# Which engine's queue issues the pair-table blocks of the six edge passes

## The chip, the cores and the metric

The program runs on one core of a Trainium2 chip. The metric is the device time of one execution in microseconds, from launch to the last output. The engines are TensorE (PE), VectorE (DVE), ScalarE (ACT), GpSimd (POOL) and SyncE (SP), which only moves data and waits. SP and ACT issue plain DMAs; POOL issues the indirect ones. All of them move through the same 16 DMA engines.

## The reference, cut to what matters

A graph of 12,500 nodes with 128 features and 200,000 edges, sorted by destination, goes through four layers, each followed by a residual and a layer norm:

```python
x = layernorm(x + L0(x, edges, w))          # W x + b, weighted neighbour sums
x = layernorm(x + L1(x, edges, attr))       # features of edges beside those of sources
x = layernorm(x + L2(x, edges, w))          # two weighted SAGE layers
x = layernorm(x + L3(x, edges, types))      # three GRU steps: msg = (h @ W_et[type])[src]; a = segment_sum(msg, dst)
```

Behind the first layer there are six sums over all edges: one for L1, two for L2, three for L3. Each is one pass below.

## The kernel before, in words

**A pass.** Each of the six passes (`ph` 1 to 6) sums rows of a table in DRAM over the edges. Most edges go by gathers. A turn has four quarters `q` of four chunks with 128 edges each. ACT copies four index columns into `stage` (line 1253) and raises `staged`; POOL issues four indirect gathers of 128 rows (line 1068), one for each column; DVE builds one-hot matrices (line 2159); PE multiplies the gathered rows by them (line 1653) and raises `summed`; DVE adds the sum to `acc` (line 2136). There are two sets of gather buffers, of even and odd turns, so ACT's copy for quarter `q` of turn `t` waits until PE has summed quarter `q` of turn `t - 2`. The profiled input takes 71 turns.

**Pair blocks.** The edges of the most frequent destinations were added earlier into two pair tables in DRAM (`PAIR_BLOCKS`), as dense weights from source tiles to groups of destinations. A pass multiplies them on PE in 196 units. A unit is one of 98 tiles of 128 source nodes and one of two halves of the table. Six units (three tiles) go with two turns: `unit(p, c)`, `c` 0 to 5. In PE's order quarter 0 is followed by no unit, quarters 1, 2 and 3 by one each. In passes 4 to 6 a unit has a block of 1 MB and four 128x512 products (line 1634), and there are two block buffers, one for each half. In passes 1 to 3 it has one field of the table, 256 KB in pieces of 256 bytes, one product (line 1637), and six buffers. Each tile also needs its rows of the node table (`dense_t` or `dense_x`). PE raises `dense_done` behind each unit.

**Who issues.** SP issues the blocks and the rows in `unit_rows` (lines 722 to 738), each behind a wait on `dense_done`. The same queue holds the loads and stores of the per-node steps (lines 801 to 842), each behind its own wait, and in pass 1 the edge features `rec` (line 743), behind waits on `summed`. All these stand in one fixed order: in passes 4 to 6 the store of types of an earlier step is ahead of unit 0 of the next pair of turns. In pass 1, blocks are asked for one turn ahead of that. At the end of a pass SP waits for all its stores before it issues the first blocks of the next.

**What stands on ACT.** ACT's order in `stage_pass` (line 1247) is four index copies a turn and, behind copies 0, 1 or 2 of some turns, the activations of a node step: `gates` (lines 1347 and 1348) behind copy 0, `new_state` (line 1353) behind copy 1, square roots behind copy 2. Before a pass ACT already waits until the table of that pass is stored.

Of the kernel before, what the change touches and what calls it, by code (L numbers as in the profile page):

```python
# [14 lines left out]
P = 128  # L15
D = 128
DE = 32
KT = 4
# [16 lines left out]
HALF = P // 2  # L35
# [61 lines left out]
def build(nc, x, src, dst, edge_attr_32, edge_type_4, edge_weight, L0_gnn_W, L0_gnn_b, L1_gnn_u, L1_gnn_W1,  # L97
# [4 lines left out]
    with ctx:  # L102
# [479 lines left out]
        def _(sp):  # L582
# [139 lines left out]
            def unit_rows(ph, table, p, c):  # L722

                half, tile = c % NH, c // NH
                unit = p * (NH * TILES) + ((ph - 1) * UNITS + c)
                at = bass.ds((p * TILES + tile) * P, P)
                if ph > 3:
                    wait(sp, dense_done, unit - 1)
                    sp.dma_start(dense_b[:, half, :, :], PAIR_BLOCKS[half][at, :, 0:KT * HALF]).then_inc(dense_in[c], 16)
                else:  # L730
                    field = (F_ONE if ph == 1 else F_W) * HALF
                    wait(sp, dense_done, unit + (1 - NH * TILES) if not isinstance(p, int) else max(unit + (1 - NH * TILES), (ph - 1) * UNITS))
                    sp.dma_start(dense_w[:, c, :, :], PAIR_BLOCKS[half][at, :, field:field + HALF]).then_inc(dense_in[c], 16)
# [12 lines left out]
            def features_in(t, unit=None):  # L746

                edge = slot_regs(mybir.EngineType.SP, edge_row, t, EP - GE)
                for q in range(NQ):
                    feature_rows(t, q, edge)  # L750
                    if unit is not None and q:
                        unit(q - 1)

            def stream_pass(ph, table, load, store, late=None):

                def body(p, units):

                    for a in range(2):
                        if a == 0 and not (isinstance(p, int) and p == 0):
                            load(p - 1)  # L760
                        if a == int(ph < 4) and not (isinstance(p, int) and p < 2):
                            store(p - 2)

                        def unit(i):
                            if a * TILES + i < units:
                                unit_rows(ph, table, p, a * TILES + i)

                        def next_unit(i):
                            if a == 0:
                                if TILES + i < units:  # L770
                                    unit_rows(ph, table, p, TILES + i)
                            elif not isinstance(p, int) or p < LEAD:
                                unit_rows(ph, table, p + 1, i)
                        if ph == 1:
                            features_in(p * 2 + a, next_unit)
                        else:
                            for i in range(TILES):
                                unit(i)
                    if late is not None and not (isinstance(p, int) and p < 2):
                        late(p - 2)  # L780
                if ph == 1:
                    for i in range(TILES):
                        unit_rows(ph, table, 0, i)
# [20 lines left out]
            def layer_pass(ph, k, loads, table, into, late=None):  # L804

                def load(m):
                    src_ = step_of(mybir.EngineType.SP, m, (NG - 1) * GN, step_src)
                    wait(sp, step_free, before(total, k, m))
                    for slot, t_ in loads:
                        sp.dma_start(by_tile(slot), node_rows_of(t_, src_)).then_inc(step_in, 16)  # L810
# [5 lines left out]
                stream_pass(ph, table, load, store, late)  # L816
                sp.wait_ge(step_out, total * (16 * (k + 1)))

            layer_pass(1, 0, [(s_xin, X1)], X1, X2)
            layer_pass(2, 1, [(s_xin, X2)], X2, H1)  # L820
# [6 lines left out]
            layer_pass(3, 2, [(s_xin, H1), (s_yin, X2)], H1, X3, types_store)  # L827
            for hh in range(2):
                sp.wait_ge(first_out[hh], total * 16)

            def state_pass(n):
# [12 lines left out]
                stream_pass(4 + n, TT[n % 2], load, store)  # L844
                if n < 2:
                    for hh in range(2):
                        sp.wait_ge(types_out[hh], total * (16 * (n + 1)))
            for n in range(3):
                state_pass(n)

# [237 lines left out]
        def _(act):  # L1088
# [158 lines left out]
            def stage_pass(ph, index, k, parts, late=None):  # L1247

                def turn(t, par, part=None, places=parts):
# [10 lines left out]
                def body(p, units):  # L1260
                    if isinstance(p, int) and p < 2:
                        turn(p * 2, 0)
                        turn(p * 2 + 1, 1)
                        return
                    g = step_of(mybir.EngineType.Activation, p - 2)
                    turn(p * 2, 0, step_parts(p - 2, g))
                    if late is None:
                        turn(p * 2 + 1, 1)
                    else:
                        turn(p * 2 + 1, 1, lambda q: late[q](p - 2, g), late)  # L1270
# [61 lines left out]
            stage_pass(1, meta_src, 0, {0: rows_turned(True), 2: step_root()})  # L1332
            act.wait_ge(step_out, total * 16)
            stage_pass(2, meta_src, 1, {0: rows_turned()})
# [6 lines left out]
            stage_pass(3, meta_src, 2, {0: rows_turned(), 2: step_root()}, {0: state_kept})  # L1341
# [13 lines left out]
            for n in range(3):  # L1355
# [5 lines left out]
                stage_pass(4 + n, meta_row, n, {0: gates, 1: new_state})  # L1361
# [1081 lines left out]
```

## Time and profile before

| | |
|---|---|
| runs | 14902.51, 14829.66, 14875.42 us; median 14875.42 |
| profiled execution | 14825.95 us |
| its span | 14824.3 us |
| granted TensorE clock, mean | 0.761 |
| DMA queue of SP (q1) | 2403570 packets, 1628.59 MB |
| indirect DMAs of POOL (q0) | 447568 packets, 628.96 MB |
| DMA queue of ACT (q10) | 31722 packets, 15.04 MB |

The page gives busy times, the waits who waited for whom, and the timeline the instructions in order of time, neighbours of one line merged. A DMA issue is a row of the queue (SPq, ACTq) and is not counted as busy; its duration is that of the issue, not of the transfer. In a merged row the duration runs from the first start to the last end, so two issues with a pause between them show the pause. "remote" is a release that the trace can't put down to an instruction. Ends of matmuls are modelled.

### The profile page before, as it was taken

To read this page: it belongs to the slowest core of one execution; us is meant where nothing else is said; L and a number is where in the kernel's file an instruction comes from. 1 tells how busy PE (TensorE), PEld (TensorE's weight loads), DVE (VectorE), ACT (ScalarE), POOL (GpSimd) and SP (SyncE) were. 2 spreads that over 40 slices of the span, in tenths; PEclk is the share of its full clock that TensorE was granted. 3 is DMA by queue.
4 is the path that set the end of the run, shared out by engine and by line. 5 is a ranking of instruction groups with operands and counts; after the bars stand their busy time and mean duration, and the time that the engine had idled before them with its cause. 6 is when DMAs were issued, how large, how long until landed. Compare 5 with 4: busy or idle time off the path is not lost. (4 is left out here: it accounts for less than half of the span.)

```text
span 14824.3 us, 166292 instructions
## 1 busy us (share of the span) xinstructions
PE 9912.4 (67%) x37230; PEld 6043.2 (41%) x37231; DVE 4854.0 (33%) x18913; ACT 1607.7 (11%) x4318; POOL 9042.1 (61%) x8448
## 2 busy tenths in 40 slices
PE   5777777886677665444445554788867888577775
PEld 3444443226545443333333333344433444344443
DVE  3333334552322222222233333233332333322224
ACT  1111112222100000000000000111100000000001
POOL 2888888770366565666656665666656666566662
PEclk6555556778777776666667777899988999788887
DMA  8999998998534332333334443666646666366663
GB/s 283 220 221 221 223 221 114 115 117 193 126 94 99 90 95 71 92 91 91 83 95 119 115 117 95 187 209 207 211 128 197 209 206 213 122 190 187 190 190 92
DMA packets 2883133, 2275.44 MB, mean 153 GB/s; under 512 B 1211014, under 2 KB 2655107, under 8 KB 2882796
## 3 DMA queue, kind: packets, MB, share of 16 engines
q1 hardware_dynamic: 2403570, 1628.59, 37.2%
q0 software_dynamic: 447568, 628.96, 22.0%
q10 hardware_dynamic: 31722, 15.04, 0.4%
q8 instruction: 76, 1.25, 0.0%
q14 instruction: 197, 1.61, 0.0%
HBM read 1545.67 MB, written 755.00 MB: 155 GB/s over the span
## 5 line engine op out<-in xcount | busy, mean ns | idle before, releaser
L1634 PE MATMUL bank<-work 128*128 128x512 f32 x4704 | 2312.7, 636 | 581.5 <-DMA work<-t_pairs 345.3
L1068 POOL DMA_INDIRECT ring<-t_types,stage x1728 | 1669.9, 966 | 1239.3 <-ACT stage L1253 727.9
L2136 DVE TENSOR_TENSOR acc<-acc,bank 128x128 f32 x1704 | 487.4, 286 | 5402.6 <-remote 3824.9
L1043 POOL DMA_INDIRECT t_sums<-ring,stage x1136 | 1763.1, 1552 | 455.5 <-issue 273.0
L1068 POOL DMA_INDIRECT ring<-t_x,stage x1152 | 1119.9, 972 | 1410.4 <-ACT stage L1253 1071.0
L1634 PEld LDWEIGHTS bank<-work 128*128 128x128 f32 x4704 | 910.2, 204 | 1579.0 <-issue 1124.1
L1653 PE MATMUL bank<-ring 128*128 128x128 f32 x6912 | 1123.2, 307 | 574.0 <-issue 418.0
L1653 PEld LDWEIGHTS bank<-ring 128*128 128x128 f32 x6912 | 1046.8, 220 | 922.9 <-issue 797.5
L1068 POOL DMA_INDIRECT more_rows<-t_types,stage x840 | 798.6, 951 | 373.4 <-issue 256.1
L2159 DVE TENSOR_SCALAR ring<-iota_f,meta_low 128x128 f32<-128x128 f32 x4544 | 1001.4, 292 | 0.1
L1514 PE MATMUL bank<-aux 128*128 128x128 f32 x2272 | 528.8, 408 | 572.7 <-ACT aux L1193 560.7
L1637 PE MATMUL bank<-work 128*128 128x512 f32 x1176 | 742.8, 711 | 139.6 <-issue 139.1
L1057 POOL DMA_INDIRECT t_pairs<-acc,pair_stage x440 | 690.3, 1569 | 230.8 <-issue 100.8
L1068 POOL DMA_INDIRECT ring<-t_h,stage x576 | 556.6, 966 | 349.3 <-ACT stage L1253 187.6
L1514 PEld LDWEIGHTS bank<-aux 128*128 128x128 f32 x2272 | 473.0, 308 | 701.1 <-ACT aux L1193 656.6
L2159 DVE TENSOR_SCALAR ring<-iota_f,meta_low,meta_w 128x128 f32<-128x128 f32 x2272 | 660.5, 360 | 250.1 <-issue 248.5
L2034 DVE SCALAR_TENSOR_TENSOR aux<-bank,aux,upto 128x128 f32<-128x128 f32 x1136 | 331.0, 349 | 1192.7 <-PE bank L1499 1004.0
L1068 POOL DMA_INDIRECT more_rows<-t_x,stage x560 | 543.3, 970 | 265.7 <-issue 164.9
L1653 PE MATMUL bank<-ring,more_rows 128*128 128x128 f32 x3360 | 521.2, 306 | 268.7 <-issue 226.8
L1653 PEld LDWEIGHTS bank<-ring,more_rows 128*128 128x128 f32 x3360 | 492.4, 220 | 393.2 <-issue 385.6
L1564 PE MATMUL bank<-work 128*128 128x448 f32 x880 | 553.0, 717 | 120.2 <-DVE aux L2076 99.7
L1253 ACT ACTIVATE stage<-meta_src 128x4 uint32 (+1 forms) x852 | 167.6, 206 | 4199.1 <-remote 2702.3
(319 smaller groups left out, 14712.1 us busy)
## 6 DMA issues: line engine op xcount, KB each, us to landing
work<-t_pairs SPq DMA_DIRECT2D x588, 1024.0 KB
t_pairs<-acc SPq DMA_DIRECT2D x544, 648.0 KB
work<-t_pairs SPq DMA_DIRECT2D x588, 256.0 KB
t_types<-work SPq DMA_DIRECT2D x216, 512.0 KB
work<-t_types SPq DMA_DIRECT2D x294, 256.0 KB
aux<-t_pairs SPq DMA_DIRECT2D x196, 256.0 KB
work<-t_x SPq DMA_DIRECT2D x108, 256.0 KB
ring<-t_types,stage POOLq DMA_INDIRECT x1728
```

The costliest lines, as they stand in the source:

```text
L1043: pool.indirect_dma_start(TAB[k], bass.IndirectOffsetOnAxis(ap=stage[:, u:u + 1], axis=0), msg[:, u, :], None, compute_op=ALU.add).then_in ...
L1057: pool.indirect_dma_start(PAIR_ROWS[TABLE_OF[s]], bass.IndirectOffsetOnAxis(ap=pair_stage[:, u:u + 1], axis=0), pair_out[:, u, :], None, c ...
L1068: pool.indirect_dma_start(gathered[par][u], None, table, bass.IndirectOffsetOnAxis(ap=stage[:, par * U + u:par * U + u + 1], axis=0)).then ...
L1253: act.activation(stage[:, at:at + K], cols(index, t * U + q * K, K), ACT.Copy).then_inc(staged, 1)
L1514: mm = pe.matmul(bank[4 + q][:, k * P:(k + 1) * P], dups[:, q, k * P:(k + 1) * P], wx_rows[:, q, :], start=True, stop=True)
L1564: pe.matmul(o[:, 0:ROW], pair_eqs[:, r, :], pair_hot[:, r, :], start=True, stop=True)
L1634: mm = pe.matmul(o, dense_t[:, tile, k_ * D:(k_ + 1) * D], dense_b[:, half, :, k_ * HALF:(k_ + 1) * HALF], start=first and k_ == 0, stop=e ...
L1637: mm = pe.matmul(o, dense_x[:, tile, :], dense_w[:, c, :, :], start=first, stop=end)
L1653: mm = pe.matmul(bank[q][:, 0:P], gathered[par][u], hot[:, u, :], start=k_ == 0, stop=k_ == K - 1)
L2034: ins = v.scalar_tensor_tensor(out=eqs[:, u, :], in0=bank[2 + q % 2][:, k * P:(k + 1) * P], scalar=cols(srcs, c + k, 1), in1=upto[:, :], o ...
L2136: v.tensor_tensor(into, into, bank[q][:, 0:P], ALU.add).then_inc(added, 1)
L2159: ins = v.tensor_scalar(hot[:, q * K + k_, :], iota_f[:, :], low(c + k_), weight(c + k_) if weight else None, ALU.is_equal, ALU.mult if we ...
```

## The change

`unit_rows` leaves SP. ACT gets `block_rows` with the same transfers and semaphores, called from `turn` behind index copies 1, 2 and 3 (not behind copy 0, and ahead of the node-step part of the same quarter). The slots are chosen so that the buffer of the issued block is the one that PE's unit frees at the time of that copy: in passes 1 to 3 ACT issues unit `c` of pair `p` at its own turn, in passes 4 to 6 the unit two further on. The rows of passes 1 to 3 go behind the second half's block, with no wait of their own. In passes 4 to 6 the first two blocks and one set of rows go ahead of the first index copy. SP keeps loads, stores and edge features, and no longer waits for all stores at the end of each pass; the load of the first step of passes 2 and 3 waits for them, and one wait stands behind all passes.

```diff
-            def unit_rows(ph, table, p, c):        # on SP, called in turns with load, store, feature_rows
...
-                if half == 0:
-                    if ph < 4:
-                        wait(sp, dense_done, unit - 4 if not isinstance(p, int) else max(unit - 4, (ph - 1) * UNITS))
-                    sp.dma_start(dense_t[:, tile, :] if ph > 3 else dense_x[:, tile, :], table[at, :]
-                                 ).then_inc(dense_x_in[tile], 16)
...
+                def block_rows(p, c):
+                    half, tile = c % NH, c // NH
+                    unit = p * (NH * TILES) + ((ph - 1) * UNITS + c)
+                    at = bass.ds((p * TILES + tile) * P, P)
+                    if ph > 3:
+                        wait(act, dense_done, unit - 1)
+                        act.dma_start(dense_b[:, half, :, :], PAIR_BLOCKS[half][at, :, 0:KT * HALF]).then_inc(dense_in[c], 16)
+                    else:
+                        field = (F_ONE if ph == 1 else F_W) * HALF
+                        wait(act, dense_done, unit + (1 - NH * TILES) if not isinstance(p, int) else max(unit + (1 - NH * TILES), (ph - 1) * UNITS))
+                        act.dma_start(dense_w[:, c, :, :], PAIR_BLOCKS[half][at, :, field:field + HALF]).then_inc(dense_in[c], 16)
+                    if half == int(ph < 4):
+                        act.dma_start(dense_t[:, tile, :] if ph > 3 else dense_x[:, tile, :], table[at, :]
+                                      ).then_inc(dense_x_in[tile], 16)
...
+                def blocks_ahead(p, a, units, before_):
+                    def block(i):
+                        if ph < 4:
+                            c = a * TILES + i
+                            if c < units:
+                                block_rows(p, c)
+                        else:
+                            c = a * TILES + i + NH
+                            if c < NH * TILES:
+                                if c < before_:
+                                    block_rows(p - 1, c)
+                            elif c - NH * TILES < units:
+                                block_rows(p, c - NH * TILES)
+                    return block
...
                         act.activation(stage[:, at:at + K], cols(index, t * U + q * K, K), ACT.Copy).then_inc(staged, 1)
+                        if block is not None and q:
+                            block(q - 1)
                         if part is not None and q in places:
                             part(q)
```

## Rows read from the trace of the kernel before

**Rows 1.** The page's first part: busy us, share of span, instructions.

```profile
PE 9912.4 (67%) x37230; PEld 6043.2 (41%) x37231; DVE 4854.0 (33%) x18913; ACT 1607.7 (11%) x4318; POOL 9042.1 (61%) x8448
```

**Rows 2.** Windows, the six passes: stretch, length, busy us and counts, clock, DMA share.

```profile
3862.00:5682.00 1820.00, 1248.32 (x6041) 882.89 (x6042) 504.98 (x2270) 115.34 (x412) 1118.50 (x1136) 0.73 0.39 92
...
5748.00:7439.00 1691.00, 709.31 (x3308) 533.81 (x3308) 455.90 (x1616) 90.21 (x347) 1080.46 (x1136) 0.67 0.36 89
...
11090.00:12816.00 1726.00, 1342.91 (x4484) 721.80 (x4484) 523.98 (x1737) 116.16 (x382) 1090.77 (x1136) 0.90 0.63 197
...
sum 10384.00, PE 6774.97 PEld 4156.39 DVE 3090.24 ACT 765.24 POOL 6557.55; mean PE 1129.16 PEld 692.73 DVE 515.04 ACT 127.54 POOL 1092.93
```

**Rows 3.** Waits of all engines over the passes: us in total, times, longest.

```profile
POOL ring L1068 <- ACT stage L1253: 1986.6, 333, 532.2
...
PE bank L1634 <- DMA work<-t_pairs: 345.3, 88, 13.7
POOL more_rows L1068 <- ACT stage L1253: 256.8, 102, 4.4
POOL work L1068 <- ACT stage L1253: 254.5, 67, 5.3
POOL wT L1068 <- ACT stage L1253: 190.8, 56, 5.2
PE bank L1634 <- DMA work<-t_types: 131.4, 50, 10.0
...
PE bank L1649 <- DMA rec<-sorted_attributes: 32.1, 24, 3.4
```

**Rows 4.** Sources L729 and L737, SP's issues: ns min/median/max, starts.

```profile
L729 SPq DMA_DIRECT2D work<-t_pairs x588: 3/554/1325, 9281.8 to 14495.4; - x196
...
L737 SPq DMA_DIRECT2D work<-t_types x294: 2/517/3081, 9282.4 to 14492.2; - x147
```

**Rows 5.** Timeline, pass 4: start us, us, engine, line, count, idle before.

```profile
10203.53 5.92 SPq L729 DMA_DIRECT2D work<-t_pairs  x2
10203.54 0.21 ACT L1253 ACTIVATE stage<-meta_w 128x4 uint32 x1 [12.83 <-remote]
...
10204.55 0.99 POOL L1068 DMA_INDIRECT wT<-t_types,stage  x1 [3.50 <-ACT stage L1253]
...
10224.68 3.87 SPq L729 DMA_DIRECT2D work<-t_pairs  x2
...
10227.84 0.21 ACT L1253 ACTIVATE stage<-meta_w 128x4 uint32 x1 [14.20 <-remote]
...
10238.44 0.56 SPq L729 DMA_DIRECT2D work<-t_pairs  x1
...
10240.91 2.84 SPq L842 DMA_DIRECT2D t_types<-work  x2
...
10244.84 3.70 PE L1634 MATMUL bank<-work 128*128 128x512 f32 x8 [1.22 <-DMA work<-t_pairs]
...
10245.17 0.01 SPq L729 DMA_DIRECT2D work<-t_pairs  x1
```

**Rows 6.** Timeline, pass 2, same columns.

```profile
6299.85 7.16 SPq L733 DMA_DIRECT2D work<-t_pairs  x2
...
6301.02 0.95 POOL L1068 DMA_INDIRECT more_rows<-t_x,stage  x1 [0.30 <-issue]
...
6317.99 0.21 ACT L1253 ACTIVATE stage<-meta_src 128x4 uint32 x1 [14.27 <-remote]
...
6319.28 0.20 ACT L1253 ACTIVATE stage<-meta_src 128x4 uint32 x1
```

**Rows 7.** Waits of SP's queue, whole span.

```profile
SPq L842 <- DVE work L2393: 330.4, 15, 76.4
```

**Rows 8.** Timeline, ACT's weight loads at the start.

```profile
1.35 0.46 ACTq L1095 DMA_DIRECT2D ring<-in_L_gnn_W1l  x1
```

More of the change, by code:

```diff
@@ L744, in feature_rows, with features_in @@
                              S_ATTR[bass.ds(edge[q], GE), :].rearrange("(k p) f -> p k f", p=P)).then_inc(attr_in[q], 16)
-            def features_in(t, unit=None):
+            def features_in(t):
                 edge = slot_regs(mybir.EngineType.SP, edge_row, t, EP - GE)
@@ L750, in features_in, with stream_pass @@
                     feature_rows(t, q, edge)
-                    if unit is not None and q:
-                        unit(q - 1)
-            def stream_pass(ph, table, load, store, late=None):
+            def stream_pass(ph, load, store, late=None):
                 def body(p, units):
@@ L762, in body @@
                             store(p - 2)
[L764 to L773, printed above, removed]
                         if ph == 1:
[L775 to L778, printed above, removed]
+                            features_in(p * 2 + a)
                     if late is not None and not (isinstance(p, int) and p < 2):
                         late(p - 2)
-                if ph == 1:
-                    for i in range(TILES):
-                        unit_rows(ph, table, 0, i)
                 pairs_of_turns(sp, body)
@@ L802, in stream_pass, with layer_pass @@
                     late(total - 1, True)
-            def layer_pass(ph, k, loads, table, into, late=None):
+            def layer_pass(ph, k, loads, into, late=None):
                 def load(m):
                     src_ = step_of(mybir.EngineType.SP, m, (NG - 1) * GN, step_src)
-                    wait(sp, step_free, before(total, k, m))
+                    if k and isinstance(m, int) and m == 0:
+                        sp.wait_ge(step_out, total * (16 * k))
+                    else:
+                        wait(sp, step_free, before(total, k, m))
                     for slot, t_ in loads:
@@ L815, in store @@
                     sp.dma_start(node_rows_of(into, g), by_tile(s_res)).then_inc(step_out, 16)
[L816 to L820, printed above, removed]
+                stream_pass(ph, load, store, late)
+            layer_pass(1, 0, [(s_xin, X1)], X2)
+            layer_pass(2, 1, [(s_xin, X2)], H1)
             def types_store(m, last_=False):
@@ L826, in types_store @@
                     sp.dma_start(node_rows_of(TT[0], g, slice(hh * 2, hh * 2 + 2)), by_tile(first_types[hh], 2)).then_inc(first_out[hh], 16)
-            layer_pass(3, 2, [(s_xin, H1), (s_yin, X2)], H1, X3, types_store)
-            for hh in range(2):
-                sp.wait_ge(first_out[hh], total * 16)
+            layer_pass(3, 2, [(s_xin, H1), (s_yin, X2)], X3, types_store)
             def state_pass(n):
@@ L843, in store @@
                                      ).then_inc(types_out[hh], 16)
[L844 to L847, printed above, removed]
+                stream_pass(4 + n, load, store)
             for n in range(3):
                 state_pass(n)
+            sp.wait_ge(step_out, total * 48)
             def to_out(at):
@@ L1245, in _, with stage_pass, turn @@
             total = all_steps(act)
-            def stage_pass(ph, index, k, parts, late=None):
-                def turn(t, par, part=None, places=parts):
+            def stage_pass(ph, index, k, table, parts, late=None):
+                def block_rows(p, c):
[18 more added lines that the diff above has]
+                                block_rows(p, c)
+                        else:
+                            c = a * TILES + i + NH
[5 more added lines that the diff above has]
+                    return block
+                def turn(t, par, part=None, places=parts, block=None):
                     for q in range(NQ):
@@ L1260, in body @@
                 def body(p, units):
+                    before_ = LAST_UNITS if isinstance(p, int) and p == LEAD + 1 else NH * TILES
+                    even, odd = (blocks_ahead(p, a, units, before_) for a in range(2))
                     if isinstance(p, int) and p < 2:
-                        turn(p * 2, 0)
-                        turn(p * 2 + 1, 1)
+                        if ph > 3 and p == 0:
+                            for c in range(NH):
+                                block_rows(0, c)
+                            even = odd = None
+                        turn(p * 2, 0, block=even)
+                        turn(p * 2 + 1, 1, block=odd)
                         return
                     g = step_of(mybir.EngineType.Activation, p - 2)
-                    turn(p * 2, 0, step_parts(p - 2, g))
+                    turn(p * 2, 0, step_parts(p - 2, g), block=even)
                     if late is None:
-                        turn(p * 2 + 1, 1)
+                        turn(p * 2 + 1, 1, block=odd)
                     else:
-                        turn(p * 2 + 1, 1, lambda q: late[q](p - 2, g), late)
+                        turn(p * 2 + 1, 1, lambda q: late[q](p - 2, g), late, block=odd)
                 pairs_of_turns(act, body)
@@ L1331, in _ @@
                 act.wait_ge(p_l0.st[par], p_l0.st_before[par] + 16 * (NG // 2 + 1 - par))
[L1332 removed]
+            stage_pass(1, meta_src, 0, X1, {0: rows_turned(True), 2: step_root()})
             act.wait_ge(step_out, total * 16)
[L1334 removed]
+            stage_pass(2, meta_src, 1, X2, {0: rows_turned()})
             def state_kept(m, g):
@@ L1360, in _ @@
                 gates.out = (lambda i: i * 16) if n < 2 else (lambda i: total * 32)
-                stage_pass(4 + n, meta_row, n, {0: gates, 1: new_state})
+                stage_pass(4 + n, meta_row, n, TT[n % 2], {0: gates, 1: new_state})
             def state_copy(at):
```

12 lines of the change are left out of this document (1 added, 11 removed).

## The prediction

> **What bounds the kernel now.** I read the busy shares first [rows 1]. No engine is full: PE has 67% of the span, POOL 61%, ACT, which gets the new work, only 11%. The windows by pass [rows 2] say more. The six passes are 10384.0 us of the 14824.3 us span, and the change touches nothing outside them. A pass takes 1691 us (pass 2), 1726 us (pass 5) or 1820 us (pass 1), although PE is busy for 709 us in pass 2 and 1343 us in pass 5. Twice the PE work moves the pass by 2%, so PE's arithmetic doesn't set the time. POOL's 1136 gathers are the same in each. One takes 0.95 us and has 0.30 us of idle before it [rows 6], so 1136 x 1.25 = 1420 us a pass, 8520 us in six. The rest, 10384 - 8520 = 1864 us, is time in which POOL issues nothing.
>
> The waits [rows 3] say for whom: POOL waited 333 times before `ring` gathers, 102 before `more_rows`, 67 before `work` and 56 before `wT`, 558 times, each time for ACT's index copy. A handful of those are starts of passes, and one of them is 532.2 us long, so I count 550 pauses. The timeline [rows 5] shows such a pause: the gather at 10204.55 had waited 3.50 us for the copy at 10203.54, and that copy had waited 12.83 us for a release that the trace can't name. By the code it is PE's `summed`. So the bound is a loop: PE sums a quarter, ACT copies, POOL gathers 1.25 us a chunk until its permits are used up, and it pauses until PE's next sums are told. A change counts in two places: if it lets PE finish a quarter sooner, or if it puts something between `summed` and the copy.
>
> **What is taken from SP.** 588 blocks of passes 4 to 6 at a median of 0.554 us and their 294 rows at 0.517 us [rows 4]; passes 1 to 3 have as many of each by the loops, 1176 blocks and 588 rows in all. SP's own time is worth nothing, as SP isn't in the loop. What can be worth something is the moment at which a block is issued.
>
> In passes 4 to 6 PE waited 345.3 us, 88 times, for a block, and 131.4 us for rows [rows 3], 476.7 us together. In passes 1 to 3, with six buffers, no such row is among the waits, so an earlier issue gives nothing there. The 476.7 us are the ceiling of this term and 0 is its floor. Most of it is transfer, not lateness. The block issued at 10238.44 was used at 10244.84, 6.40 us later, PE waiting 1.22 us for it [rows 5]; its issue took 0.56 us and nothing held it up, so ACT could not have made it come sooner. The other kind is seen at the same place: SP issued the two type stores from 10240.91 for 2.84 us, and the next block only at 10245.17, 1.42 us after their end. SP waits 330.4 us in all, 15 times, for the types of such a store [rows 7], and a block stands behind it; ACT has no stores. But the held block is unit 0, and PE has two quarters and the gate products to do before it uses that. I take a quarter of the ceiling, near the floor: 476.7 / 4 = 119 us saved.
>
> Pass 1 has one more: PE waited 32.1 us, 24 times, for edge features [rows 3], which SP issues in turns with blocks. With the blocks gone half may go, 16 us; floor 0, ceiling 32.
>
> **What is put on ACT.** A block issue is some 0.55 us, and with two or three register instructions I take 0.65 us; where rows go with it, 0.65 + 0.52 = 1.17 us. ACT's own issues at the start took 0.46 us for a smaller transfer [rows 8], so the price on ACT isn't higher than on SP. In total that is 1176 x 0.65 + 588 x 0.52 = 1070 us on an engine that is busy for 765 us of 10384 us in the passes [rows 2]. It fits easily. A turn has 20 us of gathers, and gets three blocks, 2 to 3 us.
>
> What counts is the order. Behind a block's wait and issue stand the next index copy, the step activations, and through the copy POOL. The wait itself costs nothing in principle, as the unit that frees the buffer stands ahead of the next quarter's sums in PE's order. The issue costs if permission for block and copy come together. Then the copy, for which POOL is paused, is late by 0.65 to 1.17 us. In [rows 5] SP's issue at 10203.53 and the copy at 10203.54 are such a case: they came at the same instant. At 10224.68 and 10227.84 the issue was 3.16 us ahead of the copy, and would have been over in time. And quarter 1 has no block ahead of its copy. Of 550 pauses the ceiling is all of them with rows, 550 x 1.17 = 644 us; the floor is 0. Between "half" (the two cases above) and "few" (one slot in four has no block, and blocks are freed a few us before the sums as a rule) I take a quarter: 550 / 4 x 0.65 = 89 us added. Where several permissions come together, as at 6317.99 and 6319.28, where two copies follow in 1.3 us [rows 6], only the first one matters: POOL has 5 us of gathers from each.
>
> The parts of the node steps: gates stand behind copy 0, where no block is; `new_state` stands behind block 0 of its turn, but PE forms the products it needs after the unit that frees that block, so the issue lies beside them: 0, and 0.65 us if that cover is missing, 108 times in all, 70 us.
>
> **Edges of passes.** In passes 4 to 6 two blocks and one set of rows go ahead of the first copy: 3 x (0.65 x 2 + 0.52) = 5 us. In passes 1 to 3 there are no such issues and the first blocks come later than from SP, but PE uses block 0 only after two quarters, 8 gathers or 10 us. SP's dropped waits at the ends are repeated by the wait that ACT has already: 0. Stores in SP's queue get free of blocks: they are not waited for by the loop, 0.
>
> **Sum.** -119 - 16 + 89 + 5 = -41 us against the profiled 14825.95 us, which gives 14785. That execution is 49 us below the median of the runs, 14875.42; against the median, -41 gives 14834, and I say 14835.
>
> The transfers themselves, bytes, pieces and DMA engines, stay as they are. The Trainium skill, "DMA: Bandwidth & Descriptors", section "Issuing engines are not separate DMA queues", says that DMAs from different issuing engines end up on the same 16 engines and that spreading the issue saves only the sequencer's time. By that rule the first term would be the part of the 476.7 us that is SP's lateness alone, as I have it; without it one would book the whole 476.7 us and forecast 14477. The use 6.40 us after a punctual issue [rows 5] agrees with the rule.
>
> **Rivals.** *SP is slow, and that is what PE feels.* In pass 2 two block issues took 7.16 us together [rows 6] while a single one has a median of 0.554 us [rows 4], and in the same stretch POOL and ACT go on at their usual durations. If blocks, rows and edge features come from a queue that doesn't stretch, most of PE's 476.7 + 32.1 us may go, and the pauses with them. For it: the 5.92 us and 3.87 us of pairs of issues in pass 4 [rows 5]. Against: an issue also looks late when PE's `dense_done` is told late, and ACT would see it as late; and pass 2, where SP stretches most, has no PE wait on blocks at all. Two thirds of 509 us less the 94 us of costs is -245, with a few pauses fewer -300: 14575 us.
>
> *The copies are late.* The slower side, by one mechanism: PE's releases come in bunches, so that block and copy are permitted together, as at 10203.53. If that is so at half of the pauses, and half of these blocks carry rows (mean 0.91 us), 275 x 0.91 = 250 us are added; with the block term at its floor and 5 us of edges the time is 14875 + 255 = 15130 us. It decides from about (119 + 16) / 0.91 = 150 delayed pauses, 27% of the 550. For it: the instant shared by both in one of the two cases. Against: the other case, and copy 1.
>
> *ACT gets as slow as SP.* If what stretches SP's issues comes with issuing, ACT takes 3.6 us instead of 0.65 us for a block (half of 7.16 us), 11 us a turn, and copies stand behind that. At 3 us a turn over 6 x 71 = 426 turns that is +1280 us: 16150 us. Nothing shows ACT stretched in these passes, but it issues nothing there.
>
> The Trainium skill, "Perfetto Trace Analysis", section on the HWDGE DMA instruction, has a rule that speaks against the change: the two issuing sequencers share one descriptor generator, which is locked for one of them at a time. SP's remaining stores and ACT's blocks could then hold each other up. No row here shows both queues issuing at once in a pass. It would make the second rival's price larger, by up to one issue.
>
> **Chances.** The forecast, own range 14740 to 14930: 0.46. SP's slowness 0.25, late copies 0.22, a slow ACT 0.04, the rest 0.03. I take 0.5% as what a measurement of this kernel can tell from no change; that is 74 us, so the line is at 14801 and 14950. The forecast gives 0.12 of its chance to faster, 0.31 to same and 0.03 to slower. With the rivals: faster 0.37, same 0.34, slower 0.29. The range for 8 in 10 reaches into both rivals, from 14510 to 15130.
>
> **What would show it.** In the profile after, q10 carries the blocks and rows and q1 the rest; the block issues are ACTq rows of 0.5 to 0.6 us. Right, if PE's waits for `t_pairs` fall from 345.3 by less than half, the passes stay within 1% of [rows 2], and POOL's waits for the copy stay near 550 with a little more length each. The first rival shows as PE's waits near 0 and shorter passes, pass 1 most. The second shows as POOL's pauses up by 0.5 us each with an ACTq issue right ahead of the copy. The third shows as ACTq rows stretched to microseconds. I am wrong as well if passes 1 to 3 move by over 1%, where I book almost nothing.

## The result, and the profile after

The kernel after takes 14951.74 us (median of 5 runs, 14938.77 to 14988.88), the kernel before 14868.64 us in the same comparison (14824.13 to 14902.51). The ratio is 1.0065, 95% interval 1.0046 to 1.0083. That is 83 us more by the medians, where 41 us less was forecast. Three further comparisons of the same two kernels gave 1.0054 [1.0036, 1.0072], 1.0055 [1.0038, 1.0071] and 1.0058 [1.0039, 1.0077]. The profiled execution after took 14957.69 us, its span is 14956.0 us.

The windows by pass of after, answering to [rows 2] (stretch, length, busy us and counts, clock, DMA share, GB/s; from a pass's first gather to its last):

```profile
3838.00:5687.00 1849.00, 1221.16 (x6052) 874.27 (x6052) 509.54 (x2287) 120.09 (x414) 1120.35 (x1136) 0.73 0.39 91
5748.00:7442.00 1694.00, 721.72 (x3308) 550.93 (x3308) 463.46 (x1619) 91.69 (x350) 1080.33 (x1136) 0.67 0.35 89
...
11178.00:12913.00 1735.00, 1353.88 (x4468) 725.08 (x4468) 523.46 (x1727) 115.41 (x377) 1089.09 (x1136) 0.89 0.63 196
...
sum 10541.00, PE 6801.67 PEld 4194.03 DVE 3094.64 ACT 772.01 POOL 6549.34; mean PE 1133.61 PEld 699.00 DVE 515.77 ACT 128.67 POOL 1091.56
```

The six passes are 10541.0 us against 10384.0 us: more than the whole loss is in them. PE has 0.4% more busy time and POOL 0.1% less; what grew is the time in which both wait. POOL's idle part is 10541 - 8520 = 2021 us by the count of the prediction, where it was 1864 us. Of the 157 us, 65 are in passes 1 to 3 (5291 us against 5226 us, 1.2%), which the prediction named as a sign of being wrong.

The sources of ACT's issues (ns min/median/max), answering to [rows 4]:

```profile
L1217 ACTq DMA_DIRECT2D work<-t_pairs x588: 547/561/649, 9318.5 to 14634.0; - x196
```

```profile
L1223 ACTq DMA_DIRECT2D work<-t_types x294: 536/541/1972, 9319.1 to 14624.9; - x147
```

The issue costs on ACT what was said, 0.561 and 0.541 us at the median. In passes 4 to 6 no block's issue takes over 0.65 us; single issues of rows take up to 1.97 us. The waits over the passes, answering to [rows 3]:

```profile
POOL ring L1029 <- ACT stage L1247: 1646.3, 357, 89.4
...
PE bank L1636 <- DMA work<-t_pairs: 416.6, 91, 15.2
...
POOL work L1029 <- ACT stage L1247: 272.8, 73, 5.2
...
POOL more_rows L1029 <- ACT stage L1247: 257.9, 90, 5.4
...
PE bank L1636 <- DMA work<-t_types: 156.5, 51, 6.7
...
POOL wT L1029 <- ACT stage L1247: 103.1, 27, 5.9
```

PE's waits for blocks did not fall from 345.3 us, they are 416.6 us; those for rows went from 131.4 to 156.5 us. These are single profiles: the three other profiles of the kernel after have 291.9 to 396.3 us for blocks, a second one of the kernel before (14711.06 us, on the chip called B below) 244.3 us, and 206.5 us for rows. Only the 32.1 us for edge features are gone. POOL's waits for a copy stay near 550 (357 + 73 + 90 + 27 = 547). Their sum can't be set against [rows 3] as it stands, as that holds one of 532.2 us at the start of the passes.

The timeline of after in pass 4 shows what is new (start us, us, engine, line, what, idle before; ACT and POOL, DVE's addition of a sum and PE's next unit):

```profile
9701.96 0.56 ACTq L1217 DMA_DIRECT2D work<-t_pairs  x1
9702.25 0.29 DVE L2138 TENSOR_TENSOR acc<-acc,bank 128x128 f32 x1 [7.55 <-remote]
...
9702.72 0.20 ACT L1247 ACTIVATE stage<-meta_w 128x4 uint32 x1 [8.99 <-remote]
9702.96 0.55 ACTq L1217 DMA_DIRECT2D work<-t_pairs  x1
...
9703.68 1.35 ACTq L1223 DMA_DIRECT2D work<-t_types  x1
9703.72 1.00 POOL L1029 DMA_INDIRECT work<-t_types,stage  x1 [4.38 <-ACT stage L1247]
...
9705.23 0.20 ACT L1247 ACTIVATE stage<-meta_w 128x4 uint32 x1 [2.31 <-issue]
...
9708.54 3.78 PE L1636 MATMUL bank<-work 128*128 128x512 f32 x4 [11.32 <-DMA work<-t_pairs]
```

POOL stood still for 4.38 us for the copy at 9702.72, and that copy began 0.20 us (register instructions) behind the end of a block's issue that began at 9701.96. The copy at 9705.23 again begins 0.20 us behind an issue, of rows, but POOL had four gathers to do and lost nothing by it. Where a copy ends a pause of over 1 us and its row follows on an ACT issue with nothing but register instructions between (0.2 us of them, in about a third of the cases 0.5 us), I call it held: in the profile after 88 are (24, 22 and 41 of them in passes 4, 5 and 6, one in pass 1), in the three other profiles of the same kernel 69, 84 and 69; in the kernel before, where ACT issues nothing, none. The issues ahead of them, with their register instructions, take 74 us, and 64, 78 and 67 us in the others. That is the most by which these copies can be late, as a copy's own release may have come while the issue ran. A count that asks for a copy to begin behind the issue's end, by 0.6 us at most, gives 81, 62, 73 and 61 (81, 64, 74 and 64 us), so the numbers are good to some 15%. Copies with a table load between issue and copy (last section) are not among them; that is 9 to 15 more in each profile, all in pass 4.

PE's 11.32 us in the last row are not all idle time. By the modelled ends PE's last sum was over at 9697.2, but ACT's issue was released only at 9701.96, and VectorE's next additions of sums begin at 9702.25 and 9703.23. So a sum of PE's waits in this document is an upper count, of the kernel before as well as of the others.

### The profile page after: what moved, and what is told of

Read it like the earlier page. It is cut to its first block and busy times, and to the rows that moved or that the text cites. A ratio compares the mean times of both kernels' runs of the same rounds, so it can differ in the third digit from the quotient of the medians.

```text
span 14956.0 us, 166227 instructions
## 1 busy us (share of the span) xinstructions
PE 9920.8 (66%) x37230; PEld 6075.6 (41%) x37231; DVE 4856.6 (32%) x18913; ACT 1612.5 (11%) x4318; POOL 9034.3 (60%) x8448
## 5 line engine op out<-in xcount | busy, mean ns | idle before, releaser
L1636 PE MATMUL bank<-work 128*128 128x512 f32 x4704 | 2356.5, 646 | 715.7 <-DMA work<-t_pairs 416.6
L1639 PE MATMUL bank<-work 128*128 128x512 f32 x1176 | 730.2, 702 | 73.5 <-issue 72.4
```

Source lines behind the costliest of these rows:

```text
L1636: mm = pe.matmul(o, dense_t[:, tile, k_ * D:(k_ + 1) * D], dense_b[:, half, :, k_ * HALF:(k_ + 1) * HALF], start=first and k_ == 0, stop=e ...
L1639: mm = pe.matmul(o, dense_x[:, tile, :], dense_w[:, c, :, :], start=first, stop=end)
```

## The experiments

Comparisons ran on three chips, here A, B and C. The kernel before takes 14827 to 14834 us on A, 14748 to 14862 us on B and 13032 us on C; each ratio below is against the kernel before on the same chip in the same comparison. There is no profile of the kernel before on C; what is said of C is read from profiles of four edited kernels. Here are the passes of the profiles on chip A, from the first gather of a pass to the first of the next (of pass 6 to its last gather), in us, worked out from the traces:

| kernel | 1 | 2 | 3 | 4 | 5 | 6 | 1 to 3 | 4 to 6 | ratio |
|---|---|---|---|---|---|---|---|---|---|
| waits alone on ACT | 1869 | 1734 | 1803 | 1811 | 1813 | 1700 | 5406 | 5324 | 1.0005 |
| ACT issues in 1 to 3 | 1888 | 1734 | 1824 | 1820 | 1802 | 1705 | 5446 | 5327 | 1.0016 |
| the change | 1894 | 1733 | 1827 | 1860 | 1820 | 1724 | 5454 | 5404 | 1.0055 |
| time on ACT, no wait | 1895 | 1740 | 1814 | 1816 | 1812 | 1711 | 5449 | 5339 | 1.0024 |
| double time behind waits | 1889 | 1740 | 1839 | 1863 | 1856 | 1735 | 5468 | 5454 | 1.0106 |
| copies first | 1881 | 1730 | 1827 | 1874 | 1861 | 1742 | 5438 | 5477 | 1.0124 |

Each row is one profile, and one kernel's profiles differ: in the four of the change, on A, B and the first comparison, passes 1 to 3 take 5401 to 5483 us and passes 4 to 6 take 5349 to 5410 us.

### Which passes

ACT issues for the passes in `ACT_PH` and SP for the others. SP's waits at the ends of passes (1 and 2, or 3 to 5) are dropped with it, as in the change.

```diff
             def unit_rows(ph, table, p, c):
+                if ph in ACT_PH:
+                    return
...
                 def block_rows(p, c):
+                    if ph not in ACT_PH:
+                        return
```

> The other half: ScalarE issues in passes 1 to 3 alone, SyncE in passes 4 to 6. Theory A: ratio 1.000 to 1.002, as only one pause there ends behind an issue. Theory B, and any cause that lies in passes 1 to 3: 1.003 or more. The two halves should add up to 1.0065 if passes are independent.

Measured on A: 14847.35 us against 14834.15 us, ratio 1.0016 [1.0002, 1.0029].

> ScalarE issues blocks and rows in passes 4 to 6 alone, SyncE in passes 1 to 3. The whole change costs 83 us (ratio 1.0065), and passes 1 to 3 alone came to 1.0016. Theory A (the issues stand between a release and an index copy, where PE has only two buffers, so in passes 4 to 6): 60 to 75 us, ratio 1.004 to 1.005, and 80 to 90 pauses of POOL that end with a copy right behind an ACT issue. Rival B (the block's transfer is served worse from ACT's queue): the same ratio, but the pauses behind an issue would not account for it, and PE's waits for t_pairs rise from 345 to over 400 us. If the cost is spread evenly over all passes: 1.003.

Measured on C, before at 13032.38 us: 13044.92 us, ratio 1.0006 [0.9997, 1.0015]. Once more, and the change itself, on B, before at 14748.0 us:

> ScalarE issues in passes 4 to 6 alone. Gave 1.0006 on the chip on which POOL never pauses. Where before takes about 14830 us, Theory A expects 1.004 to 1.005 (the whole change less the 1.0016 of passes 1 to 3) and some 88 pauses of POOL behind an ACT issue; where before takes 13030 us again, 1.0006 again.

> The change itself, once more. Two chips gave two different programs: on one (before 14834 us) POOL pauses some 80 times a pass and single SyncE and TensorE instructions take 0.7 us for long stretches; on the other (before 13032 us) POOL never pauses over 1 us and a pass takes 1390 us instead of 1680 us. Where before takes about 14830 us: 1.0065 again. Where it takes about 13030 us, Theory A (the issue costs only where POOL waits for the copy) expects 1.000 to 1.002; if the cost is in ACT's queue or in PE's waits for blocks it is 1.004 or more there too.

Measured: 14836.51 us, ratio 1.0059 [1.0039, 1.0080], with 77 held copies (82 us); the whole change in the same comparison 14834.17 us, 1.0054 [1.0036, 1.0072]. The expected rise of PE's waits for `t_pairs` to over 400 us, had ACT's queue served blocks worse, did not come here: they are 359.8 us. In the four profiles of the whole change they are 291.9 to 416.6 us, so this sign is a weak one; the next but one experiment tests the queue itself. By the ratios nearly all of the loss is from passes 4 to 6, where there are two block buffers. The two halves make 1.0075 together, more than the whole; the intervals allow it. This edit costs nothing on the chip on which POOL doesn't wait for copies (the whole change wasn't run on C). The waits of the kernel with ACT issuing in passes 4 to 6 on C:

```profile
POOL ring L1068 <- ACT stage L1289: 890.2, 58, 532.2
...
PEld bank L1678 <- DMA work<-t_pairs: 47.7, 35, 3.0
...
PE bank L1678 <- DMA work<-t_pairs: 38.6, 30, 2.8
```

58 waits of POOL before `ring` in place of 363 of the same kernel on B, and not one pause over 1 us ahead of a quarter. Nobody waits for the copy, so the issue ahead of it is free.

### The wait without the issue

SP issues everything, and ACT keeps the waits of the change. Against the change:

```diff
                     if ph > 3:
                         wait(act, dense_done, unit - 1)
-                        act.dma_start(dense_b[:, half, :, :], PAIR_BLOCKS[half][at, :, 0:KT * HALF]).then_inc(dense_in[c], 16)
```

> SyncE issues everything as before; ScalarE takes only the waits on dense_done at the places of the changed kernel, and issues nothing. Theory A says that the wait costs nothing and the issue everything: ratio 1.000 (within 0.15%). Theory C (the wait holds the copies back, since the unit ends later than I think): 1.004 or more.

Measured on A: 14831.94 us, ratio 1.0005 [0.9991, 1.0019]. The wait costs nothing within 0.2%, as the prediction had it.

### Time on ACT without its queue

SP issues everything; ACT does dummy work on a scratch tile where the change has the issues.

```diff
                         wait(act, dense_done, unit - 1)
...
+                    for i in range(3):
+                        wait(act, padded, unit * 3 + i)
+                        act.activation(pad[:, :], pad[:, :], ACT.Copy).then_inc(padded, 1)
```

> SyncE issues all blocks and rows as before; ScalarE waits at the same places as in the change and then does three dummy ACTIVATEs of 128x96 on a scratch tile, about 0.9 us, in place of the issues (0.56 us, or 1.10 us with rows, mean 0.83 us). Theory A (time on ACT between release and copy): ratio 1.005 to 1.008, as the whole change or a little more. Rival B (ACT's queue serves the blocks worse): 1.000 to 1.001, as with the waits alone. Half of each would be 1.003.

Measured on C: 13040.29 us, 1.0004 [0.9995, 1.0013]. On B, before at 14748.0 us:

> SyncE issues everything; ScalarE waits as in the change and does 0.9 us of dummy work behind each wait. Gave 1.0004 on the chip on which POOL never pauses. Where before takes about 14830 us, Theory A expects 1.005 to 1.008, the rival (ACT's queue serves the blocks worse) 1.000 to 1.001.

Measured: 14815.27 us, ratio 1.0046 [1.0028, 1.0064]. ACT's queue carries no block here, and most of the loss is back, with the lowest waits of PE for blocks and rows of any profile on A or B (409.1 us):

```profile
PE bank L1673 <- DMA work<-t_pairs: 212.7, 68, 11.6
PE bank L1673 <- DMA work<-t_types: 196.4, 66, 8.8
```

So it is time on ACT that costs, not the queue. Of the copies that end a pause of over 1 us, 42 follow on dummy work with at most 0.6 us or a table load between, all in passes 4 to 6; that is 39 us at most. Then without the `dense_done` wait ahead of the dummy work, and with six in place of three:

> SyncE issues everything; ScalarE does the three dummy ACTIVATEs of e4 at the same places, straight behind the copies of quarters 1 to 3, without the dense_done wait ahead of them. They are then over some 0.9 us behind the copy and hold no later copy. Theory A: 1.000 to 1.001 on any chip (e4 gave 1.0046 where POOL pauses). If the mere work on ScalarE costs (power, memory ports, the step activations behind it): 1.004 or more where POOL pauses.

> e4 with six dummy ACTIVATEs, about 1.8 us, behind each wait. Theory A, where POOL pauses: twice e4's 1.0046 or a little more, 1.009 to 1.014; where POOL does not pause, 1.000 to 1.004. If e4's cost has nothing to do with the length of the work: 1.005 again.

> The change itself as the anchor of this chip. Where before takes 14700 to 14900 us: 1.0055 to 1.0065. Where before takes about 13030 us: Theory A 1.000 to 1.002; the rival (cost through PE's blocks) 1.004 or more.

Measured together on A, before at 14826.79 us: no wait 14874.03 us, 1.0024 [1.0011, 1.0036]; double 14990.56 us, 1.0106 [1.0091, 1.0121]; the change 14925.26 us, 1.0055 [1.0038, 1.0071]. The work without the wait cost more than its expectation of 1.000 to 1.001, and about half of the 0.46% that the same work costs behind waits. No pause ends in a copy behind dummy work in it; with the double work 79 do, behind 151 us of it. By the table the work without the wait costs 5339 - 5324 = 15 us in passes 4 to 6 and 43 us in passes 1 to 3, whereas the double work behind waits costs 130 us in passes 4 to 6. So in passes 4 to 6 the place behind a release is what counts, and the cost grows with the time spent there. The timeline of the double work, ACT's first:

```profile
14636.43 1.85 ACT L1261 ACTIVATE pad<-pad 128x96 f32<-128x96 f32 x6 [7.57 <-remote]
14638.19 0.19 ACT L1284 ACTIVATE stage<-meta_w 128x4 uint32<-128x4 uint16 x1
```

and POOL's at the same time:

```profile
14634.79 0.95 POOL L1071 DMA_INDIRECT ring<-t_types,stage  x1 [0.30 <-issue]
14639.18 1.00 POOL L1071 DMA_INDIRECT ring<-t_types,stage  x1 [3.44 <-ACT stage L1284]
```

ACT was released at 14636.43 and did 1.85 us of dummies, the copy followed on them, and POOL's 3.44 us contain the whole of it. Why work on ACT that holds no copy costs passes 1 to 3 some 40 us stays open; one profile stands behind each row of the table, so the 40 us may be less, but the 0.24% of the whole is measured.

### Copies first

If the issue holds the copy, it should help to put it behind the next copy. Against the change:

```diff
-                        if block is not None and q:
-                            block(q - 1)
+                        if block is not None and q > 1:
+                            block(q - 2)
+                            if q == 3:
+                                block(2)
```

> The change, with blocks 0 and 1 of a turn one slot later: block 0 stands behind the copy of quarter 2, blocks 1 and 2 behind that of quarter 3. No copy but the next turn's copy 0 can be held by an issue, and the blocks are issued later by up to the time between two copies, 5 us. Theory A: the pauses behind an issue fall from 88 to under 35; if PE does not miss the blocks, ratio 1.001 to 1.003. Rival B: no lower than the 1.0065 of the change. Rival D (what decides is when PE gets its block, not when POOL gets its copy): PE's waits for t_pairs rise above 600 us and the ratio to 1.010 or more.

Measured on C: 13111.1 us, ratio 1.0057 [1.0043, 1.0070], the most that any kernel lost there. On A:

> Blocks 0 and 1 of a turn one slot later, so that only copy 0 can stand behind an issue. Cost 0.57% where before takes 13030 us, as PE's waits for types and pairs rose there. Where before takes 14700 to 14900 us, Theory A: pauses of POOL behind an issue fall from 68 to 88 to under 35, and the ratio to 1.003 or less if PE does not miss the blocks; if what decides is PE's wait for its block, 1.010 or more, with PE's waits for t_pairs and t_types above 700 us together.

Measured: 15013.47 us, 1.0124 [1.0107, 1.0141]. The 1.003 of my theory was wrong by a factor of four; the rival's number held. PE's waits, first of the change on that chip, then of this kernel:

```profile
PE bank L1636 <- DMA work<-t_pairs: 340.2, 92, 12.7
...
PE bank L1636 <- DMA work<-t_types: 201.3, 71, 6.9
```

```profile
PE bank L1638 <- DMA work<-t_pairs: 434.7, 135, 36.7
...
PE bank L1638 <- DMA work<-t_types: 299.5, 125, 13.5
```

541.5 us became 734.2 us, and the held copies did not go away either (55 in place of 84): the copy of quarter 0 now stands behind two issues. By the second count 40 are held, all of quarter 0, in place of 73; 16 copies of quarter 2 that look held began while the issue ran, behind `new_state`. With two buffers a block asked for one slot later is a block that PE waits for. So neither of the two orders that were tried is good: the copy is late in one, the block in the other.

### Rows on SP

Against the change:

```diff
-                    if half == int(ph < 4):
-                        act.dma_start(dense_t[:, tile, :] if ph > 3 else dense_x[:, tile, :], table[at, :]
-                                      ).then_inc(dense_x_in[tile], 16)
```

with SP issuing the rows behind its own wait.

> ScalarE issues the blocks alone in all passes, SyncE the rows (each behind its own wait). ScalarE's mean issue per unit falls from 0.83 to 0.56 us. Theory A: two thirds of the loss, ratio 1.004. Rival B (the 1 MB blocks on ACT's queue): the full 1.0065. If it is the rows' issues that hold the copies (they stand directly behind a block, 1.10 us together): 1.002 or less.

Measured on C only: 13076.45 us, 1.0027 [1.0016, 1.0038]. PE's waits for `t_pairs` are 187.8 us (80 times) where ACT issuing both in passes 4 to 6 had 38.6 us (30 times). None of the three expectations fits, as all were meant for a chip on which POOL pauses. But POOL does pause here: 46 times for over 1 us ahead of a quarter, in passes 4 and 5, and 40 times in passes 4 to 6 with the copies first, where the two kernels that cost nothing on C have no such pause. Passes 1 to 3 take 4487 to 4489 us in all four. So what these two edits cost on C comes with PE's waits. How the two queues together make PE's blocks later isn't shown; it wasn't run on A or B.

### What SP's own order is worth

The forecast gain was lateness of blocks in SP's queue. Two edits of the kernel before take parts of it away and leave ACT alone: the rows of passes 4 to 6 ahead of the block's wait, and, in passes 2 to 6, the stores behind the first block (`STORE_AT` is 0).

```diff
                 if ph > 3:
+                    if half == 0:
+                        wait(sp, dense_done, unit - 4 if not isinstance(p, int) else max(unit - 4, (ph - 1) * UNITS))
+                        sp.dma_start(dense_t[:, tile, :], table[at, :]).then_inc(dense_x_in[tile], 16)
                     wait(sp, dense_done, unit - 1)
...
-                if half == 0:
...
+                if half == 0 and ph < 4:
```

```diff
                             for i in range(TILES):
                                 unit(i)
+                                if stored and i == STORE_AT:
+                                    store(p - 2)
```

> The kernel before, with one order changed on SyncE in passes 4 to 6: the rows of a tile are issued ahead of the wait for the block's buffer (their own buffer is free since four units), not behind the block. If rows are late by their issue, PE's waits for t_types fall from 131 to 206 us to under 40 us and the ratio is 0.992 to 0.997; if they share the 1 MB block's transfer time, the waits move to t_pairs and the ratio is 0.999 to 1.001; if the block loses its place, 1.003.

> The kernel before, with SyncE's stores of a node step issued behind the first block of the same half turn pair and not ahead of it (passes 2 to 6). If the 330 us that SyncE waits for types (15 times) hold a block that PE misses, PE's waits for t_pairs fall by 50 to 120 us and the ratio is 0.994 to 0.998. If the held block is needed much later, 1.000. This is the half of the predicted 119 us that did not depend on ScalarE.

> Both of the last two edits. If they add up, the sum of their differences; if one wait hides the other, the larger of the two.

> The change itself. Where before takes 14700 to 14900 us: 1.0055 to 1.0065. Where before takes about 13030 us: 1.000 to 1.002 if the issue costs only where POOL waits for the copy, 1.004 or more if it costs through PE's blocks.

Measured on B, before at 14862.21 us: rows ahead 14855.12 us, 0.9996 [0.9985, 1.0008]; store behind 14838.15 us, 0.9989 [0.9979, 0.9999]; both 14854.19 us, 0.9993 [0.9982, 1.0003]; the change 14936.23 us, 1.0058 [1.0039, 1.0077]. PE's wait with rows ahead, and the two with the store behind:

```profile
PE bank L1635 <- DMA work<-t_pairs: 466.7, 128, 13.3
```

```profile
PE bank L1638 <- DMA work<-t_pairs: 281.9, 84, 13.2
...
PE bank L1638 <- DMA work<-t_types: 201.2, 56, 6.8
```

With the rows ahead no wait for `t_types` is left, but the waits for `t_pairs` hold 466.7 us, about what both came to, as its expectation had it for rows and block sharing the time of transfer. With the store behind the block the expected fall of PE's waits by 50 to 120 us did not come: they are 483.1 us together, where the profiles of the kernel before have 476.7 and 450.8 us. SP's stores ahead of a block are worth some 16 us, 31 us by the end of the interval. No version was found that clearly beats the kernel before.

## Why the prediction was wrong

**What bounds the kernel: right on chips A and B.** The loop of sums, copy and gathers set the time; whatever was put between release and copy cost time, and on C, where POOL doesn't pause, ACT's issues in passes 4 to 6 and the dummy work cost nothing. What makes releases by PE come some us late, as at 9702 above, stays open. That one chip has the loop and another not was in no row of before.

**"I take a quarter of the ceiling, near the floor: 119 us saved": this step failed.** The gain was not small, it was not there. The store with which I argued for lateness is worth some 16 us by experiment (31 us at the end of the interval), and "what can be worth something is the moment at which a block is issued" gave nothing: by the code ACT's order is no freer than SP's, as copies, gates and `new_state`, each with its wait, stand ahead of blocks as stores did on SP. Over the profiles other than those of C, PE's waits for blocks and rows together are 409.1 to 483.1 us (mean 461) in the eight in which SP issues in passes 4 to 6 with the rows behind the block, and 451.4 to 573.1 us (mean 529) in the five in which ACT issues in passes 4 to 6 at the places of the change. So PE's waits rose by 68 us where 119 us less was booked; counted from VectorE's last addition in each wait, which takes out what is only told late, it is 318 against 271 us, 47 us more. The two ranges overlap, so one profile of each would not have told it. These us are not all time of the kernel: the held copies (64 to 78 us at most) and passes 1 to 3 with ACT issuing (13 us by the medians, 24 us by the ratio) already make up the 83 us.

**"16 us" for edge features: the wait went, the time did not come back.** Its row of 32.1 us is gone from after in all four profiles, yet pass 1 is not shorter: from first gather to first gather it takes 1859 to 1910 us in the four, and 1864 to 1900 us in the seven on A, B and the first comparison in which SP issues it without dummy work on ACT. Where the time went isn't shown.

**"+89 us" for held copies: near, and partly by luck.** 550 / 4 = 138 copies at 0.65 us were assumed; 69 to 88 were held, behind 0.84 to 0.97 us each, for 64 to 78 us at most. The count was too high, the price too low, and the two errors nearly cancel. They were all but all in passes 4 to 6. The dummy work shows the mechanism by itself with SP issuing: +0.46%, 68 us, of which about half, 0.24%, stays when the work stands behind no wait, and is not explained by held copies.

**"0" for the waits:** shown, 1.0005 [0.9991, 1.0019]. **"5 us" at the edges** of the passes was not separated. **Passes 1 to 3** were booked with nothing but edge features; with ACT issuing in them alone the time is 0.16% more, and pass 3 is 21 us longer than with the waits alone, 24 us with the whole change. In pass 3 POOL pauses for over 1 us ahead of 87 to 96 quarters in the six profiles on A, B and the first comparison in which ACT issues there, and of 71 to 77 in the seven in which SP issues and ACT does no dummy work. Why, is open: at most two of its copies are held.

**The rivals.** "The copies are late" had the right mechanism and a decisive point of 150 delayed pauses, computed against a gain of 135 us. With no gain the point is at none, and 69 to 88 held copies were enough. "SP is slow, and that is what PE feels" is refuted: PE's waits stayed when the blocks left SP. Part of what spoke for it was misread: the 5.92 us and 3.87 us of [rows 5] are merged rows, two issues of 0.54 to 0.56 us with a wait for `dense_done` between. The 7.16 us of [rows 6] are two issues of 0.70 and 0.71 us with register instructions of 0.7 us between. "ACT gets as slow as SP" did not come, 0.561 us at the median, but a little of it did: in pass 2, 80 of 1987 recorded ACT instructions of after take 0.65 to 0.80 us, and none of 1061 of before. Of the two sequencers holding each other up little can be at work: the rows' issue of 1.35 us at 9703.68 ran while SP issued nothing. ACT's issues of passes 4 to 6 that overlap one of SP are 16 to 28 in the profiles of the change, with a mean of 0.67 to 0.83 us against 0.59 to 0.60 us for the others, 7 us in all at most.

**The rule that was weighed.** The Trainium skill, "DMA: Bandwidth & Descriptors", section "Issuing engines are not separate DMA queues", has the issuer's own time as all that a second issuer can save. The runs agree: moving the blocks gave nothing back. What SP's order held up by its stores was worth 0.1%, at the edge of what is measured (0.9989), against 0.5% for about the same time as dummy work on ACT (1.0046).

## What to carry to other kernels

Before moving DMA issues to an idle engine, don't count its idle share: find what each of its instructions releases, and ask which of them is waited for at the moment the issue is permitted. Here, where buffer and next work came free by events close together, up to the issue's full length went onto the loop, and putting it behind moved the lateness to the block. Test a supposed saving from the side of the old queue first, by one reordering there; it costs one kernel and would have shown here that there was little to win.

## What the runs showed of the hardware

**The same kernel takes 12% less time on one chip than on two others.** The kernel before took 13032 us on C and 14748 to 14862 us on A and B, all at medians of 11 to 29 runs. The window of pass 2 on C, of the kernel with ACT issuing in passes 4 to 6, whose pass 2 is that of before:

```profile
5388.00:6813.00 1425.00, 814.58 (x3316) 564.34 (x3316) 460.96 (x1627) 93.47 (x343) 1078.60 (x1136) 0.73 0.42 105
```

1425 us against 1691 us [rows 2], with POOL's gathers busy for the same 1079 us. The difference is in small instructions. In pass 2 of the profile before, 417 of 1378 recorded SP instructions, register instructions among them, take 0.65 to 0.80 us each (90th percentile 0.710 us); on C 2 of 1377 do (0.548 us, the length of a block's issue). VectorE shows the same, 291 against 34. ACT and POOL show no difference. On the chips that stretch small instructions POOL also pauses, and ACT issuing in passes 4 to 6 costs 0.6% in place of nothing (1.0059, 1.0006). That the one causes the other isn't shown. What makes the chips differ isn't settled by any run.

**An activation table is loaded between release and copy.** This was so before the change as well. In the timeline of after:

```profile
9716.38 1.28 ACT L1247 ACT_TABLE_LOAD   x1 [10.95 <-PE bank L1655]
9717.67 0.20 ACT L1247 ACTIVATE stage<-meta_w 128x4 uint32 x1
9719.72 1.28 ACT L1349 ACT_TABLE_LOAD   x1 [1.84 <-PE bank L1767]
```

The load sits behind the copy's wait, and a second one stands ahead of the gates, 30 times each in the kernel before, all in pass 4. Each is over twice as long as a block's issue. It counts only where POOL waits for that copy for over 1 us: on A, B and in the first comparison 3 to 16 of the 30 times in the profiles in which SP issues in passes 4 to 6 (before: 6, and 14 in the second profile), and 15 to 20 times where ACT issues there at the places of the change, as a block's issue then often stands ahead of the load. Whether the loads can be taken off the path was not tried.
